# Attention and expert kernel: q projection ahead of the expert masks, the two attention halves interleaved, softmax written straight into the diagonal blocks

## The reference, cut to what matters

```python
xn = layernorm(x)                                   # x: [8, 4096, 1024]
q  = xn @ Wq + bq                                   # 16 heads of 64
k, v = split((xn @ Wdown + bdown) @ Wup + bup)      # per head: 64 of k, 64 of v
q, k = rope(q), rope(k)                             # the same position for all heads of a token
att = softmax(einsum('bthd,btgd->bthg', q, k) / 8)  # for each token: 16 heads against 16 heads
attn = einsum('bthg,btgd->bthd', att, v) @ Wout + bout
e = argmax(softmax(xn @ router_w.T + router_b)); w = its probability
ffn = (xn @ expert_w[e].T + expert_b[e]) * w        # 8 experts, one per token
out = x + attn + ffn
```

## Time and profile before

| | |
|---|---|
| median of 3 runs | 4345.73 us (4344.71 to 4348.3) |
| profiled execution | 4347.35 us, span 4345.8 us on the slowest core |
| spans of the eight cores | 4312.5 to 4345.8 us |
| TensorE matmul busy | 1949.9 us (45%) |
| ScalarE busy | 1275.0 us (29%) |
| VectorE busy | 796.1 us (18%) |
| DMA mean | 84 GB/s |

### The profile page before, as it was taken

The page is one execution under the profiler, slowest core; times in us unless marked ns, Lnnn a source line. Parts: engine busy times, 40 slices in busy tenths (PEclk is TensorE's granted clock), DMA queues, the critical chain, the costliest instruction groups (busy, mean ns, idle before and its releaser), DMA issues.

```text
span 4345.8 us, 38377 instructions; the slowest of 8 cores (4312.5 to 4345.8 us)
## 1 busy us (share of the span) xinstructions
PE 1949.9 (45%) x16558; PEld 1583.9 (36%) x16558; DVE 796.1 (18%) x945; ACT 1275.0 (29%) x898; POOL 1.1 (0%) x10
## 2 busy tenths in 40 slices
PE   0111373553626354462727354452626364462727
PEld 0111252442525243351625243351625253351625
DVE  2111111111211121221111121221111121221111
ACT  0211514224060512315050413315050513315050
POOL 0000000000000000000000000000000000000000
PEclk9655575675858676675858576675858576675858
DMA  4445031130403021030403121130403031130403
GB/s 126 156 154 184 0 117 58 60 116 0 175 0 137 37 101 74 34 141 0 175 0 127 47 106 69 39 136 0 175 0 133 42 115 60 39 136 1 174 0 126
DMA packets 42363, 366.41 MB, mean 84 GB/s; under 512 B 5059, under 2 KB 6083, under 8 KB 24532
## 3 DMA queue, kind: packets, MB, share of 16 engines
q1 hardware_dynamic: 42196, 363.96, 23.0%
HBM read 330.39 MB, written 33.55 MB: 84 GB/s over the span
## 4 chain that ended last, share of the span: by engine, by line
PE 36%; ACT 20%; DMA 18%; DVE 10%; ACTq 8%; issue 4%; DVEq 3%; SPq 1%; POOL 0%; POOLq 0%
DMA exbuf<-exscratch 9%; ACTq L449 8%; PE psb L731 7%; PE psa L731 7%; ACT vdm L523 6%; ACT koct L518 6%; PE psb L670 5%; DMA y_f<-exw 4%; PE psb L649 3%; ACT qoct L500 3%; DMA x_t<-x 3%; PE psa L627 3%; PE psb L714 2%; DVEq L176 2%; DVE pav L408 2%
## 5 line engine op out<-in xcount | busy, mean ns | idle before, releaser
L670 PE MATMUL psb<-lat,wup_sb 128*128 128x256 bf16 x1024 | 224.5, 410 | 704.8 <-ACTq L449 704.8
L731 PE MATMUL psb<-xe,exbuf 128*128 128x256 bf16 x4096 | 481.4, 277 | 75.7 <-DMA exbuf<-exscratch 75.4
L731 PE MATMUL psa<-xe,exbuf 128*128 128x256 bf16 x4096 | 472.5, 274 | 0.0
L731 PEld LDWEIGHTS psb<-xe,exbuf 128*128 128x128 bf16 x4096 | 400.4, 99 | 147.1 <-issue 93.3
L470 ACT ACTIVATE lnv<-mv,epsc 128x2 f32<-128x2 f32 x16 | 4.7, 295 | 1464.9 <-DVEq L176 1464.9
L670 PEld LDWEIGHTS psb<-lat,wup_sb 128*128 128x128 bf16 x1024 | 141.0, 142 | 786.2 <-issue 728.5
L731 PEld LDWEIGHTS psa<-xe,exbuf 128*128 128x128 bf16 x4096 | 403.0, 98 | 48.5
L500 ACT ACTIVATE qoct<-psb 64x2048 bf16<-64x2048 f32 x32 | 278.7, 8710 | 223.7 <-PE psb L649 223.5
L518 ACT CAST koct<-psb 128x2048 bf16<-128x2048 f32 x32 | 278.2, 8692 | 124.2 <-PE psb L670 124.2
L523 ACT CAST vdm<-psb 64x2048 bf16<-64x2048 f32 x32 | 278.3, 8696 | 120.9 <-PE psb L670 120.9
L417 DVE TENSOR_TENSOR xe<-xnf,mrep 128x2048 bf16<-128x2048 bf16 x96 | 117.6, 1225 | 899.9 <-PE psa L731 899.9
(11 more groups left out here) (117 smaller groups left out, 1907.9 us busy)
## 6 DMA issues: line engine op xcount, KB each, us to landing
exbuf<-exscratch SPq DMA_DIRECT2D x128, 2048.0 KB, 8.5
y_f<-exw SPq DMA_DIRECT2D x64, 512.0 KB
exscratch<-exbuf SPq DMA_DIRECT2D x8, 2048.0 KB, 8.2
x_t<-x SPq DMA_DIRECT2D x32, 512.0 KB, 7.2
out<-outsb SPq DMA_DIRECT2D x32, 512.0 KB, 3.4
y_f<-wq SPq DMA_DIRECT2D x8, 512.0 KB
y_f<-wo SPq DMA_DIRECT2D x8, 512.0 KB
y_f<-wup SPq DMA_DIRECT2D x2, 1024.0 KB
```

The source lines that it names most:

```text
L670: li = tensor.matmul(out=psb[:, 256 * gch:256 * (gch + 1)], lhsT=wup[:, 4096 * k + 128 * ch: 4096 * k + 128 * (ch + 1)], rhs=lat[:, 256 * ...
L731: li = tensor.matmul(out=pout(m), lhsT=exbuf[:, eb + 1024 * k + 128 * m: eb + 1024 * k + 128 * (m + 1)], rhs=xe[:, xb + 256 * k:xb + 256 * ...
```

## The change

- In TensorE's list, q comes right after the router, ahead of prepA and prepB.
- The two halves of attention are interleaved: TensorE runs vT0, qk0, vT1, qk1, av0, av1, and ScalarE vst0, extr0, vst1, exp0, extr1, exp1, of0, of1. `vst` is twice as large, one part for each half, and av0 goes to `psb`, av1 to `psa`.
- The tile `pn32` and ScalarE's step `sca` are gone. VectorE multiplies straight into the diagonal blocks of `pdiag`, in four instructions of 32 partitions each.
- The tile `outsb` is gone. The result is added in place into `x_t` and written from there; SP waits for the output of pass i - 2 before it loads x of pass i, and VectorE no longer waits for the old output. A drain stands before the signal.
- The constants of the start that used `outsb` as scratch now use `y_f`, so the first weight load waits for them (`sync.wait_ge(smV, 2)`).

```diff
-T_SLOTS = ['xnT', 'router', 'prepA', 'prepB', 'q', 'lat', 'kv0', 'kv1', 'kv2', 'kv3',
-           'vT0', 'qk0', 'av0', 'vT1', 'qk1', 'av1', 'wout', 'expert', 'yT']
+T_SLOTS = ['xnT', 'router', 'q', 'prepA', 'prepB', 'lat', 'kv0', 'kv1', 'kv2', 'kv3',
+           'vT0', 'qk0', 'vT1', 'qk1', 'av0', 'av1', 'wout', 'expert', 'yT']
...
-        vst = e(nc.sbuf_tensor("vst", [128, 2048], BF16))
+        vst = e(nc.sbuf_tensor("vst", [128, 4096], BF16))
...
-        irow = outsb[:, 0:128]
+        irow = y_f[:, 1024:1152]
...
 # VectorE, sct and pav
-                    r3 = r16[:].unsqueeze(2).broadcast_to([128, 16, 32])
-                    vector.tensor_tensor(out=re(pn32[:], "p (o c) -> p o c", c=32),
-                                         in0=re(pex32[:], "p (o c) -> p o c", c=32),
-                                         in1=r3, op=ALU.mult)
+                    for a in range(4):
+                        srcn = re(pex32[32 * a:32 * a + 32, :], "p (o c) -> p o c", c=32)
+                        r3 = r16[32 * a:32 * a + 32, :].unsqueeze(2)
+                        dstn = re(pdiag[32 * a:32 * a + 32, :], "p (o x) -> p o x",
+                                  x=128)[:, :, 32 * a:32 * a + 32]
+                        vector.tensor_tensor(out=dstn, in0=srcn,
+                                             in1=r3.broadcast_to([32, 16, 32]),
+                                             op=ALU.mult)
                     vector.drain()
                     vinc()
-                    vector.wait_ge(smS, sv(i, 'sca%d' % w))
...
 # VectorE, yadd
-                if i > 0:
-                    vector.wait_ge(so, 32 * i)
                 for g in range(2):
-                    vector.tensor_tensor(out=outsb[:, 1024 * g:1024 * (g + 1)],
+                    vector.tensor_tensor(out=x_t[:, xo + 1024 * g:xo + 1024 * (g + 1)],
...
+                vector.drain()
                 vinc()
...
 # ScalarE, the order of one pass after kv3ev
+                scalar.wait_ge(smT, tv(i, 'vT0'))
...
+                scalar.wait_ge(smT, tv(i, 'qk0'))
...
+                scalar.wait_ge(smT, tv(i, 'vT1'))
...
+                scalar.wait_ge(smV, vv(i, 'sm0'))
+                scalar.activation(out=pex32[:], in_=p32[:], func=AF.Exp)
+                sinc(scalar.drain())
+                scalar.wait_ge(smT, tv(i, 'qk1'))
...
+                scalar.wait_ge(smV, vv(i, 'sm1'))
+                scalar.wait_ge(smV, vv(i, 'sct0'))
+                scalar.activation(out=pex32[:], in_=p32[:], func=AF.Exp)
+                sinc(scalar.drain())
+                scalar.wait_ge(smT, tv(i, 'av0'))
+                if i > 0:
+                    scalar.wait_ge(smT, tv(i - 1, 'wout'))
...
+                scalar.wait_ge(smT, tv(i, 'av1'))
...
 # TensorE: q moved from behind prepB to behind the router; then
+                tensor.wait_ge(smS, sv(i, 'vst0'))
+                tensor.wait_ge(smV, vv(i, 'qkb'))
...
+                tensor.wait_ge(smS, sv(i, 'extr0'))
...
+                tensor.wait_ge(smS, sv(i, 'vst1'))
...
+                tensor.wait_ge(smV, vv(i, 'pav0'))
...
+                tensor.wait_ge(smV, vv(i, 'pav1'))
+                tensor.wait_ge(smS, sv(i, 'extr1'))
...
+                tensor.wait_ge(smS, sv(i, 'of0'))
                 tensor.wait_ge(smS, sv(i, 'of1'))
...
 # SP
             vc = 2
+            sync.wait_ge(smV, 2)
...
                 if i >= 2:
-                    sync.wait_ge(smV, vv(i - 2, 'yadd'))
+                    sync.wait_ge(so, 32 * (i - 1))
...
                     dma(out_d[TOK * i + 128 * g:TOK * i + 128 * (g + 1), :],
-                        outsb[:, 1024 * g:1024 * (g + 1)], sem=so)
+                        x_t[:, xo + 1024 * g:xo + 1024 * (g + 1)], sem=so)
```

More of the change, by code:

```diff
@@ new lines, in _ @@
+                sinc()
+                scalar.wait_ge(smT, tv(i, 'av1'))
+                for hl in range(2):
+                    for a in range(4):
+                        srco = re(psa[64 * hl:64 * hl + 64, :],
+                                  "p (aa ol jl cc two) -> p two aa cc ol jl",
+                                  ol=16, jl=2, cc=8, two=2)[:, hl, a]
+                        dsto = re(o_f[64 * hl:64 * hl + 64, :],
+                                  "p (cc ww ol aa jl) -> p ww aa cc ol jl",
+                                  ww=2, ol=16, aa=4, jl=2)[:, 1, a]
+                        scalar.copy(out=dsto, in_=srco)
@@ L632, in _ @@
                 tinc(li)
+                for m in range(8):
+                    for k in range(8):
+                        li = tensor.matmul(out=psb[:, 256 * m:256 * (m + 1)],
+                                           lhsT=wq[:, 1024 * k + 128 * m:
+                                                   1024 * k + 128 * (m + 1)],
+                                           rhs=xnf[:, 256 * k:256 * (k + 1)],
+                                           start=(k == 0), stop=(k == 7))
+                tinc(li)
                 tensor.wait_ge(smV, vv(i, 'router'))
@@ new lines, in _ @@
+                tensor.wait_ge(smV, vv(i, 'vb'))
+                tensor.wait_ge(smS, sv(i, 'latev'))
+                tensor.wait_ge(smV, vv(i, 'mrep'))
+                for ol in range(16):
+                    li = tensor.transpose(out=psa_bf[:, 64 * ol:64 * (ol + 1)],
+                                          in_=vdm[:, 128 * ol:128 * (ol + 1)],
+                                          identity=idbf[0:64, 0:64])
+                tinc(li)
+                tensor.wait_ge(smS, sv(i, 'vst0'))
@@ new lines, in _ @@
+                tensor.wait_ge(smV, vv(i, 'qkb'))
+                for ol in range(16):
+                    li = tensor.matmul(out=psa[:, 128 * ol:128 * (ol + 1)],
+                                       lhsT=qoct[:, 128 * ol:128 * (ol + 1)],
+                                       rhs=koct[:, 128 * ol:128 * (ol + 1)],
+                                       start=True, stop=True)
+                tinc(li)
+                tensor.wait_ge(smS, sv(i, 'extr0'))
+                for ol in range(16):
+                    og = 16 + ol
+                    li = tensor.transpose(out=psa_bf[:, 64 * ol:64 * (ol + 1)],
+                                          in_=vdm[:, 128 * og:128 * (og + 1)],
+                                          identity=idbf[0:64, 0:64])
@@ new lines, in _ @@
+                tinc(li)
+                tensor.wait_ge(smS, sv(i, 'vst1'))
+                for ol in range(16):
+                    og = 16 + ol
+                    li = tensor.matmul(out=psa[:, 128 * ol:128 * (ol + 1)],
+                                       lhsT=qoct[:, 128 * og:128 * (og + 1)],
+                                       rhs=koct[:, 128 * og:128 * (og + 1)],
+                                       start=True, stop=True)
+                tinc(li)
+                tensor.wait_ge(smV, vv(i, 'pav0'))
@@ new lines, in _ @@
+                for ol in range(16):
+                    for a in range(4):
+                        li = tensor.matmul(
+                            out=psb[:, 512 * a + 32 * ol:512 * a + 32 * (ol + 1)],
+                            lhsT=vst[32 * a:32 * a + 32, 128 * ol:128 * (ol + 1)],
+                            rhs=pav[32 * a:32 * a + 32,
+                                    128 * ol + 32 * a:128 * ol + 32 * a + 32],
+                            start=True, stop=True,
+                            tile_position=(32 * a, 0))
@@ new lines, in _ @@
+                tinc(li)
+                tensor.wait_ge(smV, vv(i, 'pav1'))
+                tensor.wait_ge(smS, sv(i, 'extr1'))
+                for ol in range(16):
+                    for a in range(4):
+                        li = tensor.matmul(
+                            out=psa[:, 512 * a + 32 * ol:512 * a + 32 * (ol + 1)],
+                            lhsT=vst[32 * a:32 * a + 32,
+                                     2048 + 128 * ol:2048 + 128 * (ol + 1)],
+                            rhs=pav[32 * a:32 * a + 32,
+                                    128 * ol + 32 * a:128 * ol + 32 * a + 32],
+                            start=True, stop=True,
+                            tile_position=(32 * a, 0))
```

132 lines of the change are left out of this document (45 added, 87 removed).

## The result

The changed kernel takes 4078.4 us (median of 8 runs, 4071.1 to 4092.1), the kernel before 4346.3 (8 runs). The ratio is 0.9387, with an interval of 0.937 to 0.9404: 268 us faster. The forecast was 4092 in a range of 4035 to 4150. Its profiled execution took 4066.5 us, 12 under the median, so the trace flatters it a little.

What follows compares the result with a forecast made beforehand. A serial relay of engines, repeated 16 times, was taken to bound the kernel. 5.5 (q) + 10.9 (attention) - 0.1 (drains) = 16.3 us a pass, x 16 = 261; 4345.8 - 261 + 6.7 = 4091.7, so 4092, range 4035 to 4150.

Steps and rivals of the forecast that it cites:

- The relay: Whole token loop: engines take turns, so a microsecond off any leg is a microsecond per pass, 16 passes.
- q ahead of the masks: Router to q copy: q starts 6.4 us earlier, loses 0.9 to a colder clock, net 5.5 us a pass.
- without them q has 5.6 to 8.6 us of cold time: q projection without the mask matmuls' 1.8 us head start: takes 9.4 to 10.9 us, middle 10.1, against 9.2 before.
- rival 1: q projection: the router warms the clock, q takes 6.6 us, not 10.1; 56 us more gained, 4036; chance 0.07.
- rival 2: q projection: q stays cold to its end, 13.1 us; 48 us lost, 4140; chance 0.08.
- The masks under the copy of q: After the router: mask steps, up to 8.9 us, and latent projection end inside ScalarE's 17.4 us copy of q.
- The attention: First V transpose to output projection: 31.8 us instead of 42.7, a gain of 10.9 us a pass.
- my bounds of 0.61 and 0.77: Spacing of the four narrow VectorE multiplies: 2.5 us in all at 0.61, 3.0 at 0.77; 3.0 was taken.
- What hangs on the attention's end: After the attention: its 10.9 us a pass counted whole in the sum, with the expert stage unchanged.
- x, output, expert loads: SP's queue: old-output wait met on arrival, VectorE's 8.8 us wait for x stays, expert loads still behind x loads.
- Rivals 3 to 5: Multiplies at scattered price: 4274, 0.07; expert weights later: 4495, 0.03; ScalarE held otherwise, reordered q buys nothing: 4180, 0.03.
- The start: Kernel start: first weight load waits for VectorE's constants, 6.7 us added once; first cast about 17.7 instead of 11.0.

Runs made afterwards that it cites:

- multiplies_same_partitions: The changed kernel with all four multiplies on partitions 0 to 31, three of four groups of diagonal blocks left out; 4081.1 us.
- three_together: The changed kernel with next x loaded before the third expert load, exp0 before the second V transpose's copy, start constants' scratch in `xn_t`; 3942.4 us, ratio 0.9063.

## Why the prediction was right, step by step

- **The relay.** Right. Each leg moved gave its time whole, and alone or together the same (105 + 163 = 268).
- **q ahead of the masks.** The gap: 6.67 us measured, 6.4 predicted. The step "without them q has 5.6 to 8.6 us of cold time" fell. I had counted the mask matmuls as a head start toward the warm clock; q lost nothing without them (9.12 for 9.26, not 10.1 for 9.2), and its clock rose 4.1 us after its start, not 5 to 9. That term is 1.0 us a pass too dear, 16 us in all, the largest error of the sum. By the medians the forecast was 14 us high; by the profiled executions, of which the changed one lies 12 under its median, it was 22.
- **The router as a warm-up** (rival 1). Fell: 0.50 through the router, and q as long behind idle time as behind it. If the router were the sustained activity of which the Trainium skill speaks (TensorE: Matmul & The Clock Gate, "Part 1: The HAM clock gate"), q would have been near 6.6 us; the trace does not agree with that reading. That q stays cold throughout (rival 2) fell as well.
- **The masks under the copy of q.** Right: the mask copy was done 13.3 us before its end, the latent projection 9.5.
- **The attention.** 31.7 us measured, 31.8 predicted, and that close partly by luck, since two errors cancel: the multiplies took 2.77 us each time instead of 3.0, 0.46 less in all, and the handovers were 0.4 longer in sum (the longest miss: 0.34 us from the second transpose to av1 on the mean, not 0.2). Between my bounds of 0.61 and 0.77 the spacing was 0.69: no overlap and no gap. The Trainium skill (VectorE: DVE Perf Modes, "Two Vector instructions with no wait between them") lets a held instruction start when all before it have ended, so four of 0.69 in a row, 2.8 us, would have been the estimate by it; multiplies_same_partitions, with 0.60 on one group, agrees.
- **What hangs on the attention's end.** The prediction carried its gain on to the first expert whole. 0.44 us a pass of it came back in the projection, and of the direct multiply's own share most (0.7 to 0.9 of 1.0 to 1.1 us). This I did not foresee, and it is the reason why one part of the change is worth nothing that can be measured by itself.
- **x, output, expert loads.** Right: the wait for the old output costs nothing, the wait for x stayed (15.4 from addition to next transpose for 15.2), the expert stage is the same.
- **Rivals 3 to 5.** Fell: the multiplies are 0.69 apart, not 2.2; an expert load takes 8.9 us to landing in the median where it took 8.5, and the expert stage did not grow; ScalarE starts the copy of q with q's end.
- **The start.** 6.7 predicted; the first cast came 7.1 later, the first transpose of the first pass 3.9 on the mean over cores (425.4 to 429.3). That pair alone flatters the start: over the three kernels with the old start the mean is 423.3, over the ten with the new one 430.2, a difference of 6.9, and three_together is back at 425.0.

In sum the change gave 17.5 x 16 - 4 = 276 us by the traces and 268 by the medians, where 254 were predicted.

## What to carry to other kernels

In a relay between engines, add up the chain with its handovers; here 31.8 us was added up and 31.7 measured. But carry the sum on to the next stage that TensorE fills: where the granted clock is 0.50 at its start, as here, a microsecond gained just before may come back there, so time each small part on its own. And look at what the next pass waits for before anything else: one load moved up in SP's queue gave nearly half as much as the whole change.

## What the runs showed of the hardware that was not expected

- The output projection started up to 1.8 us earlier in some kernels than in others (attention 30.9 to 32.8 us), and the first expert came 43.5 to 44.1 us after the first V transpose in all of these that had no matmuls added. The later the projection began, the shorter it was (12.5 to 12.7, 12.0 to 12.3 and 11.3 us for the attention of 30.9, 31.7 and 32.8).
- Ahead of that projection the granted clock left 0.50 at one of two moments, 35 to 37 or 38 to 41 us after the first V transpose, and an earlier start of the projection did not bring either forward. It was the second in 16 passes of 120 with 32.8 us of attention, in 39 to 61 with 31.7, and in 46 and 68 with 30.9.
- Four VectorE multiplies of 32 x 512, each on another group of partitions, follow each other every 0.69 us; on the same group every 0.60.
- Seven microseconds of router matmuls left the granted clock at 0.50, and the mask matmuls ahead of q did not shorten its cold time (4.3 us with them, 4.1 without).
- After 38 matmuls that brought it up, the clock stood at 1.00 through 3.6 us in which TensorE did nothing. In 40 passes of 120 the same matmuls did not bring it up in time for the projection.
